# Attention scores as three single-pass products of high and low parts, with the MLP input spilled to memory

## The reference, cut to what matters

```python
h = concatenate([x, latents], axis=1)                 # 375 + 112 = 487 rows
q = (latents @ q_w + q_b).reshape(b, 112, 16, 32)
kv = (h @ kv_w + kv_b).reshape(b, 487, 16, 32, 2)     # keys and values
attn = einsum('bkhd,bnhd->bhkn', q, kmat) / 32        # the scores
attn = softmax(where(full_mask, attn, -inf))
out = rmsnorm(einsum('bhkn,bnhd->bkhd', attn, v) @ out_w + out_b + latents)
out = gelu(out @ mlp_w1 + mlp_b1) @ mlp_w2 + mlp_b2 + latents
```

## Time and profile before

| | us |
|---|---|
| timed runs, median (lowest to highest) | 895.05 (893.74 to 895.39) |
| the profiled execution's own time | 889.38 |
| its span in the profile | 887.6 |
| TensorE matmul busy | 852.0 (96%) |
| TensorE weight loads busy | 665.5 (75%) |
| VectorE busy | 572.4 (64%) |
| ScalarE busy | 429.9 (48%) |
| Pool busy | 228.9 (26%) |

### The profile page before, as it was taken

The page is one execution under the profiler, slowest core; times in us unless marked ns, Lnnn a source line. Parts: engine busy times, 40 slices in busy tenths (PEclk is TensorE's granted clock), DMA queues, the critical chain, the costliest instruction groups (busy, mean ns, idle before and its releaser), DMA issues.

```text
span 887.6 us, 16285 instructions
## 1 busy us (share of the span) xinstructions
PE 852.0 (96%) x6180; PEld 665.5 (75%) x6180; DVE 572.4 (64%) x1323; ACT 429.9 (48%) x966; POOL 228.9 (26%) x242
## 2 busy tenths in 40 slices
PE   6997999999999998999999999999999999999998
PEld 5876777777768685576877777877777777888887
DVE  4699999999999999553344443333343555545654
ACT  3313242424242445345667676657677785333442
POOL 3546555554646469200000000000000000100100
PEclk9898999999999999999999999999999999999999
DMA  8757746464555552103111101010140250000200
GB/s 332 179 128 228 189 129 158 126 155 136 145 148 146 138 156 64 56 29 107 44 54 43 54 20 46 20 46 20 52 167 11 97 198 3 0 0 13 72 0 36
DMA packets 45382, 83.11 MB, mean 94 GB/s; under 512 B 21549, under 2 KB 28205, under 8 KB 43390
## 3 DMA queue, kind: packets, MB, share of 16 engines
q1 hardware_dynamic: 40702, 80.31, 31.1%
q10 hardware_dynamic: 4608, 1.84, 0.9%
HBM read 72.43 MB, written 9.70 MB: 93 GB/s over the span
## 4 chain that ended last, share of the span: by engine, by line
PE 48%; ACT 3%; issue 1%; DVE 1%; DVEq 0%
PE bank L1955 9%; PE bank L1942 8%; PE bank L1810 8%; PE bank L1816 8%; PE bank L1906 5%; PE bank L1898 3%; PE bank L1927 3%; PE bank L1861 3%; PE bank L1847 2%; ACT smb L1376 1%; ACT pts L1384 1%; PE bank L1553 0%; PE bank L1914 0%; DVE lat_in L987 0%; DVE rows_y L990 0%
## 5 line engine op out<-in xcount | busy, mean ns | idle before, releaser
L954 DVE CUSTOM_DVE_ANT_0 smb<-bank,mask 112x487 f32<-112x487 f32 x128 | 78.1, 659 | 126.0 <-issue 126.0
L724 DVE TENSOR_TENSOR_SCAN scan<-bank,scan 128x448 f32<-128x448 f32 x128 | 131.9, 1071 | 4.5 <-POOL scan L578 3.0
L1559 PEld LDWEIGHTS bank<-xj,front 128*128 128x128 f32 x1024 | 121.1, 198 | 11.0 <-issue 9.1
L1559 PE MATMUL bank<-xj,front 128*128 128x112 f32 x1024 | 123.5, 282 | 2.2 <-POOL xj L566 2.2
L575 POOL TENSOR_TENSOR scan<-scan,ks 128x896 f32<-128x896 f32 x64 | 124.2, 1941 | 3.9 <-DMA scan<-v_scratch 3.6
L1376 ACT ACTIVATE smb<-smb,nmax 112x487 f32<-112x487 f32 x128 | 88.3, 692 | 64.2 <-DVE nmax L954 63.7
L552 POOL TENSOR_TENSOR small<-small,neghalf 112x1 f32<-112x1 f32 x24 | 13.4, 559 | 351.0 <-DVE small L990 259.8
L731 DVE TENSOR_TENSOR scan<-scan,bank 128x896 f32<-128x896 f32 x64 | 68.7, 1076 | 1.8 <-PE bank L1559 1.0
L566 POOL TENSOR_TENSOR xj<-tmp,xa 128x448 f32<-128x448 f32 x40 | 42.4, 1062 | 82.9 <-DVE tmp L693 82.9
L1384 ACT COPY pts<-bank 122x448 f32<-122x448 f32 x128 | 58.1, 535 | 0.0
L1176 ACT ACTIVATE bank<-ws 128x448 f32<-128x448 f32 x32 | 17.5, 548 | 81.8 <-DVE scan L724 67.3
(11 more groups left out here) (211 smaller groups left out, 1751.0 us busy)
## 6 DMA issues: line engine op xcount, KB each, us to landing
scan<-v_scratch SPq DMA_DIRECT2D x64, 448.0 KB, 6.0
cx<-in_ctxt SPq DMA_DIRECT2D x8, 750.0 KB, 4.8
raw_w<-in_wbig SPq DMA_DIRECT2D x4, 1024.0 KB, 8.0
w<-in_w SPq DMA_DIRECT2D x2, 2048.0 KB, 7.9
w<-in_w SPq DMA_DIRECT2D x1, 3328.0 KB, 10.5
tail<-in_wbig SPq DMA_DIRECT2D x3, 1024.0 KB, 8.8
front<-in_wbig SPq DMA_DIRECT2D x2, 1024.0 KB, 7.9
x_f<-in_x SPq DMA_DIRECT2D x8, 224.0 KB, 6.2
```

Source lines behind the costliest of these rows:

```text
L724: n = v.tensor_tensor_scan(flat, decay, flat, 0.0, ALU.mult, ALU.add)
L954: v.tensor_tensor_reduce(sm[r], bank[r][0:T, 0:NKEY], mask_b[b % 2][:, :], -1.0 / DH, 3e38, ALU.add, ALU.min, nmax[:, h:h + 1]).then_inc(s ...
L1559: i = t_.matmul(tiles(dst)[:, m, :], w[:, k, m * P:(m + 1) * P], x[:, k, :], start=k == 0, stop=k == NT - 1)
```

## The change

The scores of sequences 1 to 6 (`SPLIT_FIRST` to `SPLIT_LAST`) become three `float32r` products of high and low parts; sequences 0 and 7 stay as they were. Pool splits the keys: the high part goes into a new buffer `kt_hi`, the low part overwrites `kt`. VectorE splits the queries of a sequence into `q_hi` and `q_lo`.

`kt_hi` takes the room of `h1`. So ScalarE writes the MLP input of sequences 0 to 5 into a small buffer `h1_part`, SP stores each to memory, and loads all six back when the scores of sequence 6 are done. Sequence 6 and 7 are written to `h1` directly. `q_hi`, `q_lo` and `h1_part` take room of the first MLP weight, of which 10 blocks instead of 13 are held early. `rwide` shares a buffer with `rows_y`. Some semaphores are merged (`ve1`, `ve2` into `row_stats`, `x1_ready` and `ve3` into `squares3`).

```diff
-W1_HELD = 13
+W1_HELD = 10
+SPLIT_FIRST, SPLIT_LAST = 1, B - 2
+H1_KEPT = B - 2
...
-        rwide = room_t.take("rwide", [T, C])
+        rwide = rows_y
...
 # SP
+            def store_h1(b):
+                sp.wait_ge(s["h1_ready"], b + 1)
+                sp.dma_start(h1_scratch[b], h1_part[:, :, :]).then_inc(s["h1_moved"], 16)
+
+            def load_h1():
+                sp.wait_ge(s["s_done"], (SPLIT_LAST + 1) * NT)
+                sp.wait_ge(s["h1_moved"], 16 * H1_KEPT)
+                for b in range(H1_KEPT):
+                    sp.dma_start(h1[:, :, b * T:(b + 1) * T], h1_scratch[b]).then_inc(s["h1_moved"], 16)
...
                     load_context(b + 2)
+                if b >= 2:
+                    store_h1(b - 2)
                 load_latents(b)
...
             sp.dma_start(b1v[:, :], a["b1"]).then_inc(s["b1_loaded"], 16)
+            store_h1(B - 3)
+            load_h1()
             load_latents(B - 1)
 # Pool
+            def keys_split(b, n):
+                p, at = b % 2, 2 * ((b - SPLIT_FIRST) * NT + n)
+                pool.wait_ge(s["kv_kept"], b * NPC + n + 1)
...
+                g.tensor_copy(kt_hi[p][:, n, :], kt[p][:, n, :]).then_inc(s["kt_split"], 1)
+                pool.wait_ge(s["kt_split"], at + 1)
+                g.tensor_tensor(kt_lo[p][:, n, :], kt[p][:, n, :], kt_hi[p][:, n, :].bitcast(F32),
+                                ALU.subtract).then_inc(s["kt_split"], 1)
+
             for b in range(B):
+                split = SPLIT_FIRST <= b + 1 <= SPLIT_LAST
+                if split:
+                    keys_split(b + 1, 0)
+                    keys_split(b + 1, 1)
+                if b:
+                    rstd(3, b - 1)
+                if split:
+                    keys_split(b + 1, 2)
+                    keys_split(b + 1, 3)
                 latents_and_bias(b)
-                rstd(3, b)
+            rstd(3, B - 1)
 # VectorE
+            def query_split(b):
+                at = 2 * (b - SPLIT_FIRST)
+                dve.wait_ge(s["qt_ready"], 1 + NT if b < Q_FIRST[1] else NQ)
+                wait(dve, "s_done", b * NT)
+                v.tensor_copy(q_hi[:, :, :], queries(b)).then_inc(s["q_split"], 1)
+                dve.wait_ge(s["q_split"], at + 1)
+                v.tensor_tensor(q_lo[:, :, :], queries(b), q_hi[:, :, :].bitcast(F32), ALU.subtract
+                                ).then_inc(s["q_split"], 1)
...
                 group_max(b, 3)
+                if b and b + 1 <= SPLIT_LAST:
+                    query_split(b + 1)
                 if real(b + 2):
                     context_low(b + 2)
                 inverse_sums(b)
+                if b == 0:
+                    query_split(1)
 # ScalarE
             def mlp_input(b):
                 act.wait_ge(s["h1T_ready"], b + 1)
...
+                if b < H1_KEPT:
+                    wait(act, "h1_moved", 16 * b)
+                    dst = h1_part
+                else:
+                    act.wait_ge(s["s_done"], (SPLIT_LAST + 1) * NT)
+                    dst = h1[:, :, b * T:(b + 1) * T]
...
             def h1_high(n):
                 first, last, sequences = H1_PARTS[n]
                 act.wait_ge(s["h1_ready"], sequences)
+                act.wait_ge(s["h1_moved"], 32 * H1_KEPT)
 # TensorE, in scores(b, k)
                 wait(pe, "pt_kept", b * NH + k * HG)
-                for r in range(HG):
-                    p = r * DH
-                    i = t_.matmul(bank[r][0:T, 0:NKEY], queries(b)[p:p + DH, k, :], kt[b % 2][p:p + DH, k, :],
-                                  start=True, stop=True)
+                if SPLIT_FIRST <= b <= SPLIT_LAST:
+                    pe.wait_ge(s["q_split"], 2 * (b - SPLIT_FIRST + 1))
+                    pe.wait_ge(s["kt_split"], 2 * ((b - SPLIT_FIRST) * NT + k + 1))
+                    for q, c in ((q_hi, kt_hi), (q_hi, kt_lo), (q_lo, kt_hi)):
+                        for r in range(HG):
+                            p = r * DH
+                            i = t_.matmul(bank[r][0:T, 0:PAD], q[p:p + DH, k, :], c[b % 2][p:p + DH, k, :],
+                                          start=q is q_hi and c is kt_hi, stop=q is q_lo)
```

More of the change, by code:

```diff
@@ L77, in build @@
         latc_scratch = dram("latc_scratch", (B, P, NT, T))
+        h1_scratch = dram("h1_scratch", (H1_KEPT, P, NT, T))
         early_scratch = dram("early_scratch", (P, 2, C))
@@ L189, in build @@
                    view("qb", TAIL + 4 * WORDS - Q_COUNT[1] * NT * T, [P, NT, Q_COUNT[1] * T])]
+        room_q = Room(qa_at + Q_COUNT[0] * NT * T, TAIL + 4 * WORDS - Q_COUNT[1] * NT * T)
+        q_hi = room_q.take("q_hi", [P, NT, T], F32R)
+        q_lo = room_q.take("q_lo", [P, NT, T], F32R)
+        h1_part = room_q.take("h1_part", [P, NT, T])
+        assert TAIL + W1_HELD * NT * P <= qa_at + Q_COUNT[0] * NT * T
         kt, vv, cx, cx_hi, cx_lo = ([None, None] for _ in range(5))
@@ L201, in build @@
         context_buffers(0, room_e, room_e)
-        kt[0] = room_f.take("kt0", [P, NT, NKEY])
+        kt_at = [room_f.at, None]
+        kt[0] = room_f.take("kt0", [P, NT, PAD])
         vv[0] = room_f.take("vv0", [P, NKT, C])
@@ L211, in build @@
         q_rows = view("q_rows", lt_at, [T, C])
-        kt[1] = room_s.take("kt1", [P, NT, NKEY])
+        kt_at[1] = room_s.at
+        kt[1] = room_s.take("kt1", [P, NT, PAD])
+        kt_lo = [view(f"kt_lo{p}", kt_at[p], [P, NT, PAD], F32R) for p in range(2)]
         vv[1] = room_s.take("vv1", [P, NKT, C])
@@ L219, in build @@
         h1_at = room_t.at
-        h1 = room_t.take("h1", [P, NT, ROWS])
+        kt_hi = [room_t.take(f"kt_hi{p}", [P, NT, PAD], F32R) for p in range(2)]
+        assert h1_at + NT * ROWS <= room_t.at
+        h1 = view("h1", h1_at, [P, NT, ROWS])
         lat_in = room_t.take("lat_in", [T, C])
@@ L549, in rstd @@
             def rstd(n, b):
-                pool.wait_ge(s[f"ve{n}"], b + 1)
+                if n == 3:
+                    pool.wait_ge(s["squares3"], 2 * b + 2)
+                else:
+                    pool.wait_ge(s[f"row_stats{n}"], 3 * b + 3)
                 buf = small[n - 1]
@@ L638, in latents_and_bias @@
                 g.tensor_tensor(lat_in[:, :], lat_in[:, :], ob_rows[0:T, :], ALU.add).then_inc(s["latob_ready"], 1)
-            for b in range(B):
+            def keys_split(b, n):
+                p, at = b % 2, 2 * ((b - SPLIT_FIRST) * NT + n)
+                pool.wait_ge(s["kv_kept"], b * NPC + n + 1)
+                if b == SPLIT_FIRST and n == 0:
+                    pool.wait_ge(s["lat_stored"], 16 * B)
+                    pool.wait_ge(s["latc_stored"], 16 * B)
+                g.tensor_copy(kt_hi[p][:, n, :], kt[p][:, n, :]).then_inc(s["kt_split"], 1)
+                pool.wait_ge(s["kt_split"], at + 1)
+                g.tensor_tensor(kt_lo[p][:, n, :], kt[p][:, n, :], kt_hi[p][:, n, :].bitcast(F32),
+                                ALU.subtract).then_inc(s["kt_split"], 1)
+            for b in range(B):
+                split = SPLIT_FIRST <= b + 1 <= SPLIT_LAST
[7 more added lines that the diff above has]
+                    keys_split(b + 1, 3)
                 latents_and_bias(b)
-                rstd(3, b)
+            rstd(3, B - 1)
             pool.wait_ge(s["b2_loaded"], 16)
@@ L659, in norm_start @@
                 v.bn_stats(stats[n - 1][:, :], src[:, :]).then_inc(s[f"row_stats{n}"], 1)
-                dve.wait_ge(s[f"row_stats{n}"], 2 * b + 1)
+                dve.wait_ge(s[f"row_stats{n}"], 3 * b + 1)
                 v.memset(waiter[:, n - 1:n], 0.0)
                 v.bn_aggr(mv[n - 1][:, :], stats[n - 1][:, :]).then_inc(s[f"row_stats{n}"], 1)
-                dve.wait_ge(s[f"row_stats{n}"], 2 * b + 2)
+                dve.wait_ge(s[f"row_stats{n}"], 3 * b + 2)
                 v.tensor_scalar(small[n - 1][:, 0:1], mv[n - 1][:, 1:2], EPS_LN, None, ALU.add
-                                ).then_inc(s[f"ve{n}"], 1)
+                                ).then_inc(s[f"row_stats{n}"], 1)
             def norm_end(n, dst, src, done, b):
@@ L962, in inverse_sums @@
                 wait(dve, "ri_ready", b)
+                wait(dve, "h1T_ready", b)
                 v.tensor_copy(rwide[:, :].rearrange("t (h d) -> t h d", h=NH),
@@ L986, in rms_start @@
                 dve.wait_ge(s["latob_ready"], b + 1)
-                v.tensor_tensor(x1[:, :], bank[7][0:T, :], lat_in[:, :], ALU.add).then_inc(s["x1_ready"], 1)
-                dve.wait_ge(s["x1_ready"], b + 1)
+                v.tensor_tensor(x1[:, :], bank[7][0:T, :], lat_in[:, :], ALU.add).then_inc(s["squares3"], 1)
+                dve.wait_ge(s["squares3"], 2 * b + 1)
                 wait(dve, "h1T_ready", b)
                 v.tensor_tensor_reduce(rows_y[:, :], x1[:, :], x1[:, :], 1.0 / C, EPS_RMS, ALU.mult, ALU.add,
-                                       small[2][:, 0:1]).then_inc(s["ve3"], 1)
+                                       small[2][:, 0:1]).then_inc(s["squares3"], 1)
             def rms_end(b):
@@ L1323, in kv_keep @@
```

(13 more changed lines are left out.)

14 lines of the change are left out of this document (6 added, 8 removed).

## The result

The changed kernel takes 900.0 us (median of 6 runs, 898.58 to 902.17); the kernel before, on the same chip, 894.61. The ratio is 1.0062, with a 95% interval of 1.0035 to 1.0089: 5.4 us slower. The forecast was 895.9, with no measurable change as the likeliest outcome (0.42, and 0.40 for slower).

The account below looks back on a forecast made before the run. TensorE was taken to bound the kernel, busy 852.0 of 887.6 us. Terms -3.5 + 0.6 + 0.55 + 0.1 + 2.8 + 0.3 = +0.85 us on 889.38, plus 5.7 to the timed median, gave 895.9; range 892.5 to 900.5.

Parts of the forecast that it names:

- Part 1: Score groups of sequences 1 to 6: three f32r rounds make 0.87 us a group instead of 1.01, -3.5 us in all.
- the second rival: Score groups: weights of rounds two and three load in the open, a group is 1.1 us; 901.4 us, chance 0.12.
- the fourth: Score groups: no packing at all, a group above 2 us, +39.5 us; chance 0.05.
- Part 2: Two more semaphore waits before each score group: +0.6 us for the six first groups, 0 for the 18 others.
- The step of 0.09: Start of score groups: first groups with four waits start 1.00 us behind the weighted sum, later ones with one 0.91.
- Part 3: Split of the queries on VectorE: +0.55 us once, before sequence 1's scores; 0 for sequences 2 to 6.
- Part 4: Split of the keys on Pool: +0.1 us in all, from delaying VectorE's low part of the attention output.
- Part 5: Spilled MLP input's late return behind w2 and b1 on the SP queue, delaying the last sequence: +2.8 us.
- The upper end of 4.5: Return of the spilled MLP input: cost in us if the sixth store takes 1.5 longer.
- Part 6: W1_HELD 10 instead of 13: second w1 load 1.9 us longer, ahead of a GELU; +0.3 us (0 to 1.5).
- the product at 738.18: TensorE product needing w2's second low part, which was counted ready near 738.4, hence +0.3 us.
- rival 3: Around the array: Pool's copy as dear as its difference (1.75 us), the return takes 4.5; 899.3 us, chance 0.18.

Follow-up runs that it names:

- spare products: Changed kernel plus TensorE products nobody reads, 13 ahead of the late transposes and 9 ahead of the last projection: 896.6 us.

## Why the prediction was right or wrong

**Part 1, the scores: right.** Forecast 0.87 a group from 0.20 and three rounds of 0.222; measured 0.855 from 0.19 and three of 0.222. That is 24 x 0.16 = 3.9 against 3.5. The row that carried it was the eight loads within 0.29 us: a row group's next weights do load while it multiplies. The rule of the Trainium skill (TensorE: Matmul & The Clock Gate, section "Part 3: Packing small matmuls — row/col tiling"), that a load overlaps a running product only in another row group, is not what this trace shows: two more rounds cost 0.445, which leaves nothing for loads in the open. With a group of 0.855 the second rival falls, and the fourth.

**Part 2, the waits: 0 instead of +0.6.** A later group starts 0.904 behind its weighted sum with three waits as with one, a first group 0.946 with six where it was 1.00 with four (four of the five in sequences 2 to 6; sequence 4 has 0.904 and had 0.939). The step of 0.09 that I read between the rows was not the price of waits; what it is, no run shows.

**Part 3, the queries: right.** 0.66 once for sequence 1 (0.55 forecast), nothing elsewhere. **Part 4, Pool: right**, nothing to be seen on TensorE; the copy took 0.59 and the difference 1.25, as taken. The sign that was to show it dear, a low part stretched past 0.5, came in five sequences, and it cost nothing: the projection wanted the result 0.6 later.

The stage of these four came out at -3.8, against -2.25 forecast (-3.5 + 0.6 + 0.55 + 0.1).

**Part 5, the way back: the right place, mis-sized: +2.8 forecast, 5.3 by the stage, 6.0 by the timed runs.** The order of events was as told: w2, b1, the store, then the loads, ScalarE, TensorE. Two sizes were off. On the scale of the trace after, which starts sequence 7 1.9 us later, the store was forecast to land near 702.2 and landed at 703.77, and the last load near 709.4 and landed at 711.38: 2.0 later. The upper end of 4.5 was set for just that, a store that takes 1.5 longer. The other is a term that the sum didn't have: TensorE's idle time put its clock to 1.2 GHz, and the 28 products behind it took 6.24 us instead of 4.32. TensorE had more slack than the few tenths I gave it (4.87 of idle on ScalarE made 3.38 on TensorE), or it would have been worse. For the queue the Trainium skill (DMA: Bandwidth & Descriptors, section "Queues, rings and completion order") says that each DMA engine consumes its descriptors in ring order; the trace agrees, with 9.0 us to landing for the store behind w2 and 2.0 ahead of it.

**Part 6, W1_HELD: the step that failed. +0.3 forecast, 3.8 by the stage, 1 to 4 by all runs.** The load itself was sized rightly: 1.9 us for the three blocks, and the GELU came 2.0 to 2.3 later. What failed is "the product at 738.18" as the first that waits: I followed the GELU through w2's low part to that product and found it a few tenths late, and named the MLP input of sequence 6 behind the GELU without asking who waits for it. It is the output projection of sequence 7, ahead of that product in TensorE's order, which started at 735.18 right behind that MLP input: no slack at all. So the delay went through whole (the GELU 2.3 later, TensorE idle 2.30), and the half clock came on top of it.

The sum was +0.85 and it became +5.4, 4.5 us too little in all, with the gain of the scores larger than forecast by 1.6 and the two waits dearer by 6. That 900.0 still lies in the range is luck: its upper end came from rival 3, which named the total (899.3), but of whose two reasons only the dear return was right; the Pool copy was not dear, and the w1 load is not among them.

## What to carry to other kernels

When a wait gets longer, list every instruction behind it on its engine, and for each the engine that waits for it; the first one without slack sets the price, not the one that the chain of the old trace happened to show. Put a late return ahead of a large load on the same queue when the load is wanted later, and a wait as near as can be to the first reader: here the two moves were worth 9.3 us by the stages, the new arithmetic 3.8. In these runs an idle TensorE of 2 to 3 us cost more than its idle time, so a price for such a gap has a second term.

## What the runs showed of the hardware

The prediction had no term for the clock, and it fell to 1.2 GHz behind short gaps: behind 3.38 and 2.30 us in the changed kernel, and with W1_HELD 10 in the kernel before behind 2.19, there only after the first 1.3 us of work. In the changed kernel 28 products took 6.24 us instead of 4.32, and 12 took 4.57 instead of 2.78; the spare products gave back some 1.5 us in each of the two stages. The same idle times don't always end the same way: near 350 us every kernel idles twice for 1.5 us, and with W1_HELD 7 the clock fell behind that (0.66 granted from 355 to 360 us), while in the changed kernel it stayed at 1.00.

Two rows of the granted clock in the run with W1_HELD 10, the idle stretch's end and the one behind it:

```profile
740.00:742.00 2.00, 1.14 (x5) 0.94 (x6) 1.63 (x4) 2.00 (x6) 0.00 (x0) 1.00 0.00 0
742.00:744.00 2.00, 2.00 (x7) 1.45 (x6) 1.15 (x2) 1.36 (x3) 0.00 (x0) 0.54 0.04 8
```
